# Exps and maxima in pairs in attention units 5 and 6 of a three-layer macaron kernel

## What is computed

```
x = x + 0.5 * ffn(layernorm(x))     # attention with 16 heads of 8, rope, then shared + routed experts
x = x + attn(layernorm(x))          # attention with 16 heads of 4 on x[..., :64]
x = x + 0.5 * ffn(layernorm(x))
```

```
left = x[..., :E // 2]
q, k, v = (left @ W.T).reshape(N, S, 16, 4)  for Wq, Wk, Wv
energy = einsum('nqhd,nkhd->nqkh', q, k)
att = softmax(energy / scale, axis=2)
out = einsum('nqkh,nkhd->nqhd', att, v).reshape(N, S, 64)
return out @ Wo.T + bo
```

## Time and profile before

| what | us |
|---|---|
| median of 3 executions | 834.25 (834.14 to 837.18) |
| profiled execution | 834.06 |
| its span | 832.0 |
| PE busy | 804.7 |
| DVE busy | 664.6 |
| ACT busy | 501.9 |
| POOL busy | 353.5 |

### The profile page before, as it was taken

How to read it: one execution, slowest core, us unless ns; L and a number is a source line. 1 busy time by engine, 2 the same in 40 slices (tenths; PEclk the granted TensorE clock), 3 DMA queues, 4 the chain that set the end, 5 groups by cost and what they waited for, 6 DMA issues and landing times. The chain is left out here.

```text
span 832.0 us, 13459 instructions
## 1 busy us (share of the span) xinstructions
PE 804.7 (97%) x4436; PEld 308.7 (37%) x4438; DVE 664.6 (80%) x1303; ACT 501.9 (60%) x1073; POOL 353.5 (42%) x760
## 2 busy tenths in 40 slices
PE   8899999999999999999999999999999999999996
PEld 3323334334333343332323232233433434355453
DVE  6999987697789758887989999988988687673355
ACT  3267664475467627765877777777764475376441
POOL 2564328615331353424442357334253623442534
PEclk9999999999999999999999999999999999999999
DMA  4565203010200010020010323204102200000000
GB/s 119 129 168 128 81 2 78 19 58 11 70 2 2 20 62 2 9 74 3 3 51 32 78 81 83 76 14 107 37 21 58 77 2 14 1 15 2 1 13 14
DMA packets 24700, 37.83 MB, mean 45 GB/s; under 512 B 6464, under 2 KB 22080, under 8 KB 23048
## 3 DMA queue, kind: packets, MB, share of 16 engines
q1 hardware_dynamic: 24149, 36.25, 15.5%
q10 hardware_dynamic: 483, 0.74, 0.3%
HBM read 27.03 MB, written 9.11 MB: 43 GB/s over the span
## 5 line engine op out<-in xcount | busy, mean ns | idle before, releaser
L1387 ACT ACTIVATE probs<-ps 128x512 f32<-128x512 f32 x768 | 414.4, 598 | 228.0 <-PE ps L957 205.1
L1178 DVE TENSOR_REDUCE maxes<-ps 128x1 f32<-128x512 f32 x768 | 479.1, 681 | 47.6 <-PE ps L924 45.5
L924 PE MATMUL ps<-k_aug,q_aug 72*128 72x512 bf16 (+1 forms) x768 | 246.2, 382 | 3.5 <-ACT k_aug L1358 0.7
L957 PE MATMUL ps<-q_aug,k_aug 75*128 75x512 bf16 (+1 forms) x704 | 231.8, 383 | 3.3 <-DMA q_aug<-maxT 1.3
L984 PE MATMUL ps_out<-probs,v_aug 128*18 128x512 f32 x1408 | 185.4, 598 | 1.7 <-ACT probs L1387 1.0
L924 PEld LDWEIGHTS ps<-k_aug,q_aug 72*128 72x128 bf16 (+1 forms) x768 | 64.3, 96 | 162.8 <-issue 107.1
L1058 PE MATMUL ps<-w,hidden 128*128 128x512 f32 x256 | 118.7, 596 | 0.0
L957 PEld LDWEIGHTS ps<-q_aug,k_aug 75*128 75x128 bf16 (+1 forms) x704 | 59.0, 97 | 136.3 <-issue 88.9
L1279 DVE TENSOR_TENSOR prod<-ps,gate 128x512 f32<-128x512 f32 x56 | 38.7, 691 | 54.5 <-PE ps L1058 43.6
L1579 POOL TENSOR_TENSOR prod<-prod 128x512 f32<-128x512 f32 x28 | 35.5, 1268 | 85.2 <-DVE prod L1279 68.8
L1499 POOL TENSOR_SCALAR max_parts<-maxes 128x16 bf16<-128x16 f32 (+1 forms) x38 | 10.9, 288 | 141.6 <-DVE maxes L1178 141.4
(11 more groups left out here) (157 smaller groups left out, 755.3 us busy)
## 6 DMA issues: line engine op xcount, KB each, us to landing
q_aug<-qk_parts SPq DMA_DIRECT2D x7, 1152.0 KB
k_aug<-qk_parts SPq DMA_DIRECT2D x21, 384.0 KB
qk_parts<-parts SPq DMA_DIRECT2D x48, 128.0 KB, 2.3
q_aug<-qk_parts SPq DMA_DIRECT2D x11, 288.0 KB
k_aug<-qk_parts SPq DMA_DIRECT2D x27, 96.0 KB
qk_parts<-parts SPq DMA_DIRECT2D x24, 64.0 KB, 2.0
X<-in_x_dram SPq DMA_DIRECT2D x4, 256.0 KB, 4.6
w<-in_ffn_W_experts_dram SPq DMA_DIRECT2D x2, 512.0 KB, 5.8
```

What stands on the lines that cost most here:

```text
L924: pe.matmul(bank(use[i]), q_aug[p0:p1, r, at, qt * 128:(qt + 1) * 128], k_aug[p0:p1, r, at, :], start=True, stop=True).then_inc(bank_full[ ...
L957: pe.matmul(bank(use[i]), k_aug[p0:p1, r, at, kt * 128:(kt + 1) * 128], q_aug[p0:p1, r, at, :], start=True, stop=True).then_inc(bank_full[ ...
L1178: dve.tensor_reduce(maxes[:, u % 2, qt, at:at + 1], full(use[0]), AX.X, ALU.max).then_inc(bank_free[use[0][0]], 1)
L1387: act.activation(probs[:, step % P_RING, c:c + exp_run(u), :], both(use), ACT.Exp, scale=scale)\
```

## The change

Two more units are put into the set of units in which exps and maxes begin in twos:

```diff
 MAX_PAIRS = set()
 EXP_PAIRS = set()
 LAST = UNITS - 1
-TOGETHER_UNITS = {4, 7}
+TOGETHER_UNITS = {4, 5, 6, 7}
 VECTOR_EXPERTS = {LAST, LAST + 1}
 P_RING = 2
 PIECES = 4
```

## The result

The changed kernel takes 841.0 us (median of 4 executions, 840.11 to 842.68) against 834.2: the ratio of the two is 1.0063, with a 95% interval of 1.0039 to 1.0088. It is slower, clear of the noise; 831.6 us had been forecast, with a range up to 838.0. Here and in all that follows, executions more than 1.5% above the fastest of their kernel stay out: three of e14 (848.3 to 855.6 us), one of e5 (1144.4 us) and one of the kernel before (1564.8 us).

The account below looks back on a forecast made before the run. TensorE, busy 804.7 of 832.0 us, was taken to bound the kernel; profiled 834.06 - 2.6 for side groups + 0.19 to the median gave 831.6 us, plain groups' 0.4 left in the error; range 826.5 to 838.

Parts of the forecast that it names:

- the term of -2.6 us for the groups with side work: Units 5 and 6, 20 groups carrying projections, transposes and experts: a gain of 2.6 us, the middle of 0 and 5.1.
- The pairing on PE: Units 5 and 6: at unit 4's 0.155 us per score matmul, pairs take 7.7 us off PE time, the gain's upper bound.
- the 19.5 and 19.8 expected: Sign to check: PE time in us of k_aug reads in units 5 and 6 after the change, from 23.88 and 23.15.
- Plain groups at a floor of 2.55 us: Twelve groups of units 5 and 6 without side work: 2.55 us against 2.58, a gain of 0.4 us left inside the error.
- Between 0 and 5.1 us from the 20 side groups, lower bound a loss of 1.1: Units 5 and 6, groups with side work: possible gain up to 5.1 us, possible loss 0.27 us per five groups.
- The comparison of five groups of unit 7 with five of unit 6: Paired groups of unit 7 took 15.23 us, unpaired ones of unit 6 14.96; used as the case against a gain.
- The slower rival: Units 5 and 6: pairs wait for an unfinished max's bank, 0.29 us in each of 32 groups; 838.4 us, chance 0.16.
- DVE, expected at 90 and 95% in units 5 and 6: Sign to check: DVE's busy share after the change, with unit 5 shorter by about 1.7 us and unit 6 by 0.9.
- Granted in full in every slice: Whole kernel: TensorE's clock was taken as fully granted, so there was no clock to win.
- The factor of 2 of the Trainium skill's page "TensorEngine Tiling (Array Packing)": Score pairs in units 5 and 6: by this rule alone all 7.7 us come back, 826.5 us; full-gain rival's chance 0.22.
- Unit 8's k rows: Transfer ahead of unit 8's first max: slack of 1.3 us or more, shrinking by 0.3, so it stays covered at zero cost.

Follow-up runs that it names:

- e14: Kernel before, with PE made to wait for one exp ahead of unit 7's v projection; median 841.3 us against 835.8, fastest 835.2 against 833.3.
- e5: The changed kernel run once more, unaltered; 837.9 to 843.9 us.
- e3: Changed kernel, same order, but the planner counts the second exp's bank in units 5 and 6 free 0.3 places later; median 837.3 us, fastest 834.4.
- e11: e3 with four side steps of PE (five places) in units 5 and 6 moved one place earlier; fastest 832.2 us.
- e15: Changed kernel with four side steps of PE (five places) moved one place earlier, without the bank repair; fastest 834.1 us.
- e9: e3 with six zero-weight matmuls in unit 5 where PE waits; time not given, six of ten executions at mean clock 0.993 or lower.
- e10: Changed kernel with six zero-weight matmuls in unit 5 where PE waits; fastest 838.2 us.
- e12: e11 with six zero-weight matmuls added in unit 5 where PE waits; 833.3 us, ratio 0.9976 to the kernel before.
- e4: Kernel before, with only the exps of units 5 and 6 beginning in pairs, maxes left spread; 840.7 us.
- e7: e3 with the weighing of v in units 5 and 6 one place later; fastest 837.2 us.
- e8: Kernel before, with the weighing of v in units 5 and 6 one place later; fastest 833.3 us.

## Why the prediction was wrong

The step that failed is the term of -2.6 us for the groups with side work, "the middle of 0 and 5.1". In its place the runs show a loss of about 4.4 us at full clock, and two costs that the sum had at nothing: banks held by a second exp, and side work that stands behind the max that waits for one. A third, the clock, adds 2.5 to 3 us at the median.

- **The pairing on PE**: 7.7 us of k_aug reads were to vanish, 2.7 did (2.0 and 0.7). The step took unit 4's rate as a property of the order. In units 5 and 6 a second max often meets a busy bank, and a torn pair saves nothing. The better bank did not bring this back either: the reads take 22.15 and 22.30 us in e3, and 21.94 and 21.90 in e11, against the 19.5 and 19.8 expected. In e3 too the last max of a plain group comes 0.4 us behind its partner. So the upper bound of 7.7 us was too high whatever the banks.
- **Plain groups at a floor of 2.55 us**: right where the bank is the first exp's (2.54 in e3), wrong where it is the second's (2.86). The floor was worked out from the chain exp, ACT, weighing, and left out that the eighth fill of a group has to come out of the same seven banks. The front of the document had the bank count, and the earlier trace rows had shown the eighth score waiting 0.62 us.
- **Between 0 and 5.1 us from the 20 side groups, lower bound a loss of 1.1**: this step failed by sign and size. A side step at the end of a group went from filling PE's wait to standing behind it (+0.85 us in the group shown); moving five of them back gave 3.9 us (e15). The comparison of five groups of unit 7 with five of unit 6 showed no gain and should have set the sum, not a middle with a gain read off PE's work.
- **The slower rival** named the right resource, a bank, and the right victim, the scores behind it, but the wrong owner: an exp still in ACT's queue, not an unfinished max. Its 838.4 us is near the 838 of the fastest executions, by luck: its price of 0.29 us was read off a group of unit 7 that waited for DVE, and was charged to all 32 groups. DVE, expected at 90 and 95% in units 5 and 6, was at 82 and 89%. The rival was given 0.16 and the range ended at it, with nothing for the clock.
- **"Granted in full in every slice"** was a misreading of the earlier trace rows: a 9 there stands for 90% or more, and the first trace has a spell from 35.1 us on, in a slice that shows 9. The clock was not thought of as something that more waiting could lose. Of the 7 us at the median, about 4.4 are there in the fastest executions (837.9 to 838.2 against 833.5 to 833.6), the other 2.5 to 3 are spells.
- **The factor of 2 of the Trainium skill's page "TensorEngine Tiling (Array Packing)"** held for pairs that run: two matmuls lie in one row of 0.39 us, and the next pair starts 0.22 us on (474.75 and 474.97). It is a factor for TensorE alone. The prediction noted that this rule says nothing of the engines that empty the banks; the page itself does, in its section "PSUM Bottleneck": tiling does not speed up the emptying of PSUM. Here getting both partners' banks at one time decided.
- **Unit 8's k rows** stayed covered: unit 7 took 50.1 us in the changed kernel (487.3 to 537.4) and 49.8 before, so no gap of that kind grew there; units 4 to 6 account for the 6.7 us.

What stays open: what of PE's activity brings a spell on. One more standing sets the spells off (e14); filling two other waits with zero matmuls of 36 rows did not stop them (e9, e10), but went with a steadier clock once the side steps were moved (e12). Whether the zeros, the few rows or the place matter wasn't tried.

## What to carry to other kernels

Count the buffers before pairing work on an in-order engine: if a group issues more fills than there are banks, the last fill waits for one of the group's own, and which of two nearly equal ones the planner gives it was worth 0.3 us a group here. Side work that fills a wait must stay ahead of the instruction that waits; after any reordering see what now stands first in the queue. When waiting grows on TensorE, compare the mean granted clock over many executions, since here a wait of 1.2 us cost over five at the median.

## What the runs showed of the hardware

One wait of 1.2 us, put into a kernel that keeps PE 97% busy, was followed by 10.2 us at half clock in the trace, and by mean clocks down to 0.979 with 847.1 us (e14). Spells began at 413.0 to 416.8 us in six traces (the changed kernel, e4, e7, e9, e10, e14), 28 to 32 us behind the start of unit 5, and at 406.0 in e11. They are not bound to that place or to the pairs: one of some 3.5 us began at 334.5 to 336.2 us, in unit 4, in six traces (the changed kernel, e7, e8, e11, e12, e14), two of which have the order of the kernel before there and in units 5 and 6 (e8 but for its weighings, and e14). A stretch of 7.2 us in which PE was 93% busy by the profile's count, with two zero matmuls in it, was followed by a spell of 10.2 us (e9).
